# A decoder layer on one core: units laid out by a table, and VectorE asks for three kinds of results one or two search rounds later

## The chip, the cores and the metric

The kernel runs on one core of a Trainium2 chip. The time is the device time of one execution in microseconds (us); shown are the median of three runs, and one execution recorded by the hardware profiler. The engines are TensorE (PE in the rows; PEld are its weight loads), VectorE (DVE), ScalarE (ACT), GpSimd (POOL) and SyncE (SP), which here only starts transfers. Each works through its own list of instructions in order and waits on semaphores for the others.

## What is computed

A decoder layer over 8 sequences of 512 rows of 512 numbers, in fp32: causal self attention with a normalization of each query and key head, cross attention of 16 heads in which each query row keeps only its 32 largest scores, and a gated MLP with quantized activations and ternary weights. Cut to what matters:

```python
x = x + attn(layernorm(x))            # 16 heads of 32, q and k normalized per head, causal softmax
x = x + xattn(layernorm(x), ctx)      # scores; top_k(scores, 32); softmax over them; times V; @ Wo.T
x = x + ffn(layernorm(x))             # 512 -> 2048 -> 512
def ffn(x):
    gate, up = silu(bitlinear(x, w_gate)), bitlinear(x, w_up)
    return bitlinear(gate * up, w_down)
def bitlinear(x, w):                  # rows scaled by max|x|, rounded to 127 steps; w to -1, 0, 1
    return act_quant(x) @ weight_quant(w).T
```

## The kernel before

After a setup of the weights (to about 140 us) the kernel is one long software pipeline written by hand. Its step is the **slot**, numbered `s` from -7 to 161. In a slot the self attention works on one query tile of 128 rows for a group of 4 heads, and the cross attention on another: self attention of item `s`, cross attention of item `c = s - LAG`, 20 slots later. A batch (sequence) is 16 slots, 4 head groups of 4 query tiles; `s % 4` is the query tile, and with the causal mask its scores grow from 128 to 512 columns.

**TensorE.** A slot has 8 cells (0 to 7), even ones for a self head, odd ones for a cross head. In each cell TensorE transposes the probabilities of the item before (`probs`, L593), makes the scores of a new one (`scores`, L625 to L630) and multiplies the last turned probabilities with V (`values`, L607). `cells(s)` (L120) then appends **units** to a cell: `self_qkv` (L682, four per group), `cross_v` (L694), `cross_kT` and `cross_qT` (L701), `self_kT` and `self_qT` (transposes), the output projections `self_oT`, `self_out`, `cross_oT`, `cross_out` (L654), the turned rows `feed` and `x2T`, and of the MLP `gate` and `up` (L662, four chunks of 512 per row tile, chunk 0 to 3), `hT` (L635) and `down` (L670). Units share two PSUM banks in turn; a unit waits until the unit two before it has been read.

**VectorE.** It finds the 32 largest scores of each row by search rounds: MAX8 gives the eight largest (L876), MATCH_REPLACE8 takes them out (L881). Each slot is two halves of two heads; a half is FIRST_MAX, ROUND_1, ROUND_2 (a replacement and a maximum for each of its heads) and ROUND_3 (with one more replacement). Between the rounds stand its other duties, in a written order: `self_maxima` (L1013), `sum_squares` (L1005), `norms` (the weighted sums of both attentions, divided by their weights, L898 and L907; it waits for TensorE's last sum of the slot before), `mlp` (maximum of a chunk of gate times up, L965; a chunk is **early** if its gate and up stand in cell 2, **late** if in cell 6, and a late one's maximum is taken in the next slot), `down` (L983), `row_scale`, `cross_rows` (adds `cross_out` to the rows, L924) and `self_rows` (adds `self_out`, L937).

**ScalarE** copies each result out of PSUM and takes the exponentials, `rest_exp` (L825) after the last replacement of a half. **GpSimd** makes the negative maxima as biases (`cross_bias` L1175, `self_bias` L1182), gate times up (`silu`, L1109 to L1115), the differences of exponentials (L1168), the quantization of the chunks (`inner_quant`, L1127), and in slots with `s % 4 == 2` the head norm (a power, L1147).

**SyncE** goes through the slots too: feeds of rows, `x1`, `x2` and residual rows, weights of a group (one buffer for both attentions), then 32 copies of the turned keys and queries into their stacks (L513), which the first scores of a group need.

The MLP of a batch follows its cross attention. **Table numbers** below count slots from the batch's first cross slot: slot number 26 is `s = LAG + 16*b + 26`, in which the next batch's cross attention is at 10. Before, `cross_tile` (projection of tile t) is at 15 + t, chunks 0, 1 of tile t at 17 + 3t, chunks 2, 3 at 18 + 3t, and `hT` with `down` at 19 + 3t. `self_tile` is the self attention's projection, for a batch two ahead at numbers 26 to 29.

## Time and profile before

| | |
|---|---|
| median of 3 runs | 3904.87 us (3895.12 to 3911.36) |
| profiled execution | 3917.24 us, its span 3915.5 us |
| mean granted TensorE clock | 0.867 of full speed |
| busy: PE, PEld | 3310.2 us (85%), 2433.7 us (62%) |
| busy: DVE, ACT, POOL | 3220.0 us (82%), 2451.7 us (63%), 1917.9 us (49%) |

The span has four parts: setup to about 140 us; self attention alone until VectorE's first search at 490.7 us; the searches of 128 items until 3771 us; and the last projections and MLP tiles. Busy time says how much an engine works, not what holds it up; for that one reads what ended each idle time. The granted clock is 1 at 2.4 GHz and 0.5 at 1.2 GHz, so a mean of 0.92 is 16% of the time at the lower level.

### The profile page before, as it was taken

To read this page: it belongs to the slowest core of one execution; us is meant where nothing else is said; L and a number is where in the kernel's file an instruction comes from. 1 tells how busy PE (TensorE), PEld (TensorE's weight loads), DVE (VectorE), ACT (ScalarE), POOL (GpSimd) and SP (SyncE) were. 2 spreads that over 40 slices of the span, in tenths; PEclk is the share of its full clock that TensorE was granted. 3 is DMA by queue.
4 is the path that set the end of the run, shared out by engine and by line. 5 is a ranking of instruction groups with operands and counts; after the bars stand their busy time and mean duration, and the time that the engine had idled before them with its cause. 6 is when DMAs were issued, how large, how long until landed. Compare 5 with 4: busy or idle time off the path is not lost.

```text
span 3915.5 us, 61337 instructions
## 1 busy us (share of the span) xinstructions
PE 3310.2 (85%) x18502; PEld 2433.7 (62%) x18502; DVE 3220.0 (82%) x7571; ACT 2451.7 (63%) x4921; POOL 1917.9 (49%) x2444
## 2 busy tenths in 40 slices
PE   1577888999989998999999989999899988877765
PEld 1355567766666676667667667667666766554542
DVE  4311189999989999899989998999989998999961
ACT  2344466676777677667766677767666776555533
POOL 0122334446555466546654655546554654355445
PEclk7677878898999989988989999988998898887768
DMA  8112232232223222322223222322233221211100
GB/s 279 46 49 65 80 84 73 74 82 75 51 76 88 75 69 79 84 79 74 76 72 84 75 52 74 87 76 67 79 88 83 65 71 41 62 46 36 33 22 19
DMA packets 167443, 283.04 MB, mean 72 GB/s; under 512 B 40639, under 2 KB 52939, under 8 KB 166606
## 3 DMA queue, kind: packets, MB, share of 16 engines
q1 hardware_dynamic: 160782, 275.98, 25.9%
q10 hardware_dynamic: 6336, 3.15, 0.3%
q8 instruction: 153, 2.51, 0.3%
q14 instruction: 172, 1.41, 0.1%
HBM read 113.27 MB, written 31.46 MB: 37 GB/s over the span
## 4 chain that ended last, share of the span: by engine, by line
DVE 33%; PE 32%; POOL 11%; issue 8%; ACT 6%; SPq 4%; DMA 1%; DVEq 0%; POOLq 0%; ACTq 0%
DVE cW L881 15%; DVE top L876 12%; PE bank L682 6%; PE bank L607 6%; PE bank L654 5%; SPq L513 4%; PE bank L593 3%; PE bank L670 2%; PE bank L701 2%; PE bank L635 2%; POOL hh L1111 2%; POOL srs L1147 2%; POOL hh L1115 2%; PE bank L694 2%; DVE smx L1013 2%
## 5 line engine op out<-in xcount | busy, mean ns | idle before, releaser
L881 DVE MATCH_REPLACE8 cW<-top,cW 128x512 f32<-128x512 f32 x1536 | 1026.3, 676 | 0.0
L876 DVE MAX8 top<-cW 128x8 f32<-128x512 f32 x1536 | 980.7, 680 | 0.0
L1168 POOL TENSOR_TENSOR cS<-cS,cW 128x512 f32<-128x512 f32 x512 | 642.2, 1276 | 233.2 <-ACT cW L825 232.7
L797 ACT ACTIVATE PT<-bank 128x512 f32<-128x512 f32 (+3 forms) x1024 | 538.0, 525 | 314.4 <-PE bank L593 310.6
L607 PE MATMUL bank<-cv,PT 128*128 128x33 f32 x4096 | 586.0, 290 | 121.8 <-ACT PT L797 120.6
L607 PEld LDWEIGHTS bank<-cv,PT 128*128 128x128 f32 x4096 | 555.0, 210 | 157.0 <-ACT PT L797 151.0
L1175 POOL TENSOR_SCALAR cnb<-top 128x2 f32<-128x2 f32 x256 | 49.3, 193 | 871.6 <-DVE top L876 857.9
L607 PEld LDWEIGHTS bank<-sv,PT 128*128 128x128 f32 x2560 | 398.7, 211 | 77.7 <-ACT PT L797 55.4
L825 ACT ACTIVATE cW<-cW,cnb 128x512 f32<-128x512 f32 x512 | 347.8, 734 | 127.6 <-DVE cW L881 127.2
L819 ACT ACTIVATE cS<-cS,cnb 128x512 f32<-128x512 f32 x512 | 380.1, 742 | 46.9 <-POOL cnb L1175 24.0
L682 PE MATMUL bank<-w_group,xT 128*128 128x384 f32 x1024 | 403.3, 541 | 0.0
L607 PE MATMUL bank<-sv,PT 128*128 128x33 f32 x2560 | 374.5, 281 | 32.4 <-ACT PT L797 31.5
L1013 DVE TENSOR_REDUCE smx<-sP 128x2 f32<-128x256 f32 (+3 forms) x256 | 205.7, 804 | 225.9 <-ACT sP L806 225.9
L593 PE MATMUL bank<-ident,cS 128*128 128x128 f32 x2048 | 346.2, 296 | 0.0
L881 DVE MATCH_REPLACE8 cW<-top,cS 128x512 f32<-128x512 f32 x512 | 342.1, 676 | 0.3 <-issue 0.3
L876 DVE MAX8 top<-cS 128x8 f32<-128x512 f32 x512 | 327.0, 680 | 7.6 <-ACT cS L806 7.6
L806 ACT ACTIVATE cS<-bank 128x512 f32<-128x512 f32 x512 | 312.7, 611 | 1.8 <-PE bank L630 1.8
L812 ACT ACTIVATE sP<-sP,snb 128x384 f32<-128x384 f32 (+3 forms) x512 | 294.1, 577 | 28.3 <-POOL snb L1182 27.3
L593 PEld LDWEIGHTS bank<-ident,cS 128*128 128x128 f32 x2048 | 279.5, 162 | 46.0 <-issue 23.5
L682 PEld LDWEIGHTS bank<-w_group,xT 128*128 128x128 f32 x1024 | 201.7, 207 | 133.9 <-issue 34.2
L593 PE MATMUL bank<-ident,sP 128*128 128x128 f32 x1280 | 254.6, 301 | 35.8 <-ACT sP L812 34.8
L1161 POOL TENSOR_TENSOR part<-part 128x512 fp32r<-128x512 f32 x128 | 163.1, 1274 | 243.1 <-ACT part L740 242.8
(151 smaller groups left out, 6131.8 us busy)
## 6 DMA issues: line engine op xcount, KB each, us to landing
sk_stack<-part SPq DMA_DIRECT2D x512, 64.0 KB, 2.0
sq_stack<-part SPq DMA_DIRECT2D x512, 64.0 KB, 2.0
ck_stack<-part SPq DMA_DIRECT2D x512, 64.0 KB, 2.0
cq_stack<-part SPq DMA_DIRECT2D x512, 64.0 KB, 2.0
w_group<-wa_by_group SPq DMA_DIRECT2D x32, 768.0 KB, 4.8
w_group<-wc_by_group SPq DMA_DIRECT2D x32, 768.0 KB, 4.3
feed<-in_x SPq DMA_DIRECT2D x32, 256.0 KB, 3.0
feed<-in_ctx SPq DMA_DIRECT2D x32, 256.0 KB, 3.0
```

Source lines behind the costliest of these rows:

```text
L593: mm = pe.transpose(turned_ps[C.parity("turned_full", label)][:, k * P:(k + 1) * P], p[:, k * P:(k + 1) * P], ident[:])
L607: mm = pe.matmul(o[:, j * (HD + 1):(j + 1) * (HD + 1)], pt[:, k * P:(k + 1) * P], v[m // NT % len(v)][:, k, j, :], start=k == 0, stop=k == ...
L682: mm = pe.matmul(ps[:, 0:3 * P], xT[:, c, t * P:(t + 1) * P], w_group[:, c, :], start=False, stop=c == NC - 1, skip_group_check=True)
L797: act.activation(PT[k][:, 0:n], turned_ps[k][:, 0:n], ACT.Copy).then_inc(turned_read, step("turned_read", label))
L806: act.activation(dst, score_ps[k][:, 0:n], ACT.Copy).then_inc(score_read, step("score_read", label))
L812: act.activation(p, p, ACT.Exp, bias=snb[:, j:j + 1], scale=SCALE).then_inc(sexp, step("sexp", (m, j)))
L819: act.activation(cS[c % 2][j][:], cS[c % 2][j][:], ACT.Exp, bias=cnb[c % 2][:, j:j + 1], scale=SCALE).then_inc(cexp, step("cexp", (c, j)))
L825: act.activation(cW[j][:], cW[j][:], ACT.Exp, bias=cnb[c % 2][:, j:j + 1], scale=SCALE).then_inc(crest, step("crest", (c, j)))
L876: dve.max(top8[:, j, r, :], src[:]).then_inc(topk, step("topk", (c, r, "max", j)))
L881: dve.match_replace(cW[j][:], top8[:, j, r, :], src[:], REPLACED).then_inc(topk, step("topk", (c, r, "replace", j)))
L1013: dve.reduce_max(smx[:, 2 * half:2 * half + 2], sP[half][:, :, 0:n], AXX).then_inc(smax, step("smax", (s, half)))
L1168: pool.tensor_tensor(cS[m % 2][j][:], cS[m % 2][j][:], cW[j][:], ALU.subtract).then_inc(cprob, step("cprob", (m, j)))
```

## The change

The places of the units come from a function `schedule(b)` with lists of table numbers, and so do `hT` (now `mlp_inner`) and `down`, which may be in different slots. For most batches `cross_tile` is at 15, 17, 18, 19, the 16 chunks are spread over 20 to 33 (one or two a slot, some slots with none), `hT` is at 22, 25, 30, 35 and `down` at 23, 25, 30, 37. The last two batches keep groups of three slots a tile. The first `self_qkv` of a group moves from cell 0 to cell 5 of the slot before; others move by a cell. On VectorE the second self maximum moves behind ROUND_1, `norms` behind ROUND_2, `cross_rows` behind ROUND_3, the first self maximum behind ROUND_1 and `self_rows` behind ROUND_2 of the second half. GpSimd's late `silu` goes ahead of the self bias, ScalarE's first two cross exponentials one cell earlier. SyncE's row transfers move behind the stack copies, their loads a slot ahead. The amount of work is the same: VectorE has 3961 merged rows in either kernel.

```diff
+def schedule(b):
+
+    def dense(first):
+        chunks = [(first + 3 * t + r, early) for t in range(NT) for r in range(2) for early in (True, False)]
+        ends = tuple(first + 3 * t + 2 for t in range(NT))
+        return chunks, ends, ends
+    if b == NB - 1:
+        return ((15, 16, 17, 18), *dense(17))
+    if b == NB - 2:
+        return ((15, 17, 18, 19), *dense(20))
+    chunks = [(20, True), (20, False), (21, True), (21, False), (22, False), (23, True), (24, True), (24, False),
+              (26, True), (27, True), (29, True), (29, False), (31, True), (32, True), (32, False), (33, True)]
+    return (15, 17, 18, 19), chunks, (22, 25, 30, 35), (23, 25, 30, 36 if b == NB - 3 else 37)
...
+def planned(s, part, entry, tiles=NT):
+
+    out = []
+    for b in range(NB):
+        for i, at in enumerate(schedule(b)[part]):
+            if at == entry(s - LAG - SLOTS * b):
+                out.append(tiles * b + i)
+    return out
...
 def cells(s):
 
     u = [[] for _ in range(CELLS)]
-    g, q = self_group(s), s % NT
+    q = s % NT
+    g = s // NT + 2
+    if q == 3 and 0 <= g < NGROUPS:
+        u[5].append(("self_qkv", g, 0))
+    g = self_group(s)
     if g is not None:
-        for at, cell, unit in ((0, 0, ("self_qkv", g, 0)), (0, 3, ("self_qkv", g, 1)), (0, 6, ("self_qkv", g, 2)),
-                               (1, 1, ("self_qkv", g, 3)), (3, 2, ("self_kT", g)), (3, 3, ("self_qT", g))):
+        for at, cell, unit in ((0, 2, ("self_qkv", g, 1)), (0, 5, ("self_qkv", g, 2)),
+                               (1, 0, ("self_qkv", g, 3)), (3, 2, ("self_kT", g)), (3, 3, ("self_qT", g))):
             if at == q:
                 u[cell].append(unit)
     g = cross_group(s)
     if g is not None:
-        for at, cell, unit in ((1, 5, ("cross_v", g)), (2, 0, ("cross_kT", g)), (2, 3, ("cross_qT", g))):
+        for at, cell, unit in ((1, 5, ("cross_v", g)), (2, 0, ("cross_kT", g)), (2, 4, ("cross_qT", g))):
             if at == q:
                 u[cell].append(unit)
     if cross_tile(s) is not None:
         u[0].append(("cross_oT", cross_tile(s)))
         u[1].append(("cross_out", cross_tile(s)))
     if x1_tile(s) is not None:
-        u[1].append(("feed", "x1", x1_tile(s)))
+        u[2].append(("feed", "x1", x1_tile(s)))
     if self_tile(s) is not None:
-        u[2].append(("self_oT", self_tile(s)))
-        u[3].append(("self_out", self_tile(s)))
+        u[4].append(("self_oT", self_tile(s)))
+        u[5].append(("self_out", self_tile(s)))
     if x2_tile(s) is not None:
         u[4].append(("x2T", x2_tile(s)))
+    for t in mlp_inner(s):
+        for n in range(NF):
+            u[3 + n].append(("hT", t, n))
...
                     for s in slots:
                         c = s - LAG
                         top(c, 0, FIRST_MAX)
+                        top(c, 0, ROUND_1)
                         self_maxima(s - 1, 1)
-                        top(c, 0, ROUND_1)
                         sum_squares(s)
-                        norms(s)
                         mlp(s - 1, False)
                         down(s - 1)
                         top(c, 0, ROUND_2)
+                        norms(s)
                         row_scale(s)
+                        top(c, 0, ROUND_3)
                         cross_rows(s)
-                        top(c, 0, ROUND_3)
                         top(c, 1, FIRST_MAX)
+                        top(c, 1, ROUND_1)
                         self_maxima(s, 0)
-                        self_rows(s)
-                        top(c, 1, ROUND_1)
                         feed_stats_of(s + 1)
                         top(c, 1, ROUND_2)
+                        self_rows(s)
                         mlp(s, True)
                         top(c, 1, ROUND_3)
...
                         cross_bias(c, 0)
+                        silu(s - 1, False)
                         self_bias(s - 1, 1)
-                        silu(s - 1, False)
                         for j in (2, 3):
                             probability(c - 1, j)
                         low_parts(now[0] + now[1] + now[2])
                         rows_quant(s)
                         inner_quant(s - 1)
                         head_norm(s)
-                        low_parts(now[3])
+                        low_parts(now[3] + now[4])
...
                         elif k == 1:
+                            cross_exp(c, 0)
+                        elif k == 2:
+                            cross_exp(c, 1)
                             self_exp(s - 1, 2)
-                        elif k == 2:
+                        elif k == 3:
                             self_exp(s - 1, 3)
-                            cross_exp(c, 0)
-                        elif k == 3:
-                            cross_exp(c, 1)
```

VectorE in the slot of table number 29, from the second half's first maxima (cS_2 and cS_3 are the scores of its two heads, cW what is left of them); before:

```order
L876 MAX top<-cS_2 128x8
L876 MAX top<-cS_3 128x8
L1013 TENSOR_REDUCE smx<-sP 128x2
L937 TENSOR_TENSOR xres<-bank,xres 128x512
L940 BN_STATS x1stat<-xres 128x6
L944 BN_AGGR x1mv<-x1stat 128x2
L881 MATCH_REPLACE cW<-top,cS_2 128x512
L881 MATCH_REPLACE cW<-top,cS_3 128x512
L876 MAX top<-cW 128x8 x2
```

and now:

```order
L901 MAX top<-cS_2 128x8
L901 MAX top<-cS_3 128x8
L906 MATCH_REPLACE cW<-top,cS_2 128x512
L906 MATCH_REPLACE cW<-top,cS_3 128x512
L901 MAX top<-cW 128x8 x2
L1038 TENSOR_REDUCE smx<-sP 128x2
L906 MATCH_REPLACE cW<-top,cW 128x512 x2
L901 MAX top<-cW 128x8 x2
L962 TENSOR_TENSOR xres<-bank,xres 128x512
L965 BN_STATS x1stat<-xres 128x6
L969 BN_AGGR x1mv<-x1stat 128x2
L990 TENSOR_REDUCE hmx<-hh 128x1
```

The self maximum moved behind one round and the addition of `self_out` (xres) behind two; an early chunk's maximum (hmx) follows it.

TensorE in the same slot, around `self_out` (wproj, oT); before, from its bias on:

```order
L651 MATMUL bank<-bias,ones 128x512
L654 MATMUL bank<-wproj,oT 128x512 x4
L593 MATMUL bank<-ident,sP 128x128
L625 MATMUL bank<-sk_stack,sq_stack 128x256
L627 MATMUL bank<-mask,ident 128x128
L607 MATMUL bank<-cv,PT 128x33 x4
L593 MATMUL bank<-ident,cS_2 128x128 x4
L630 MATMUL bank<-ck_stack,cq_stack 128x512
L607 MATMUL bank<-sv,PT 128x33
L692 MATMUL bank<-bias,ones 128x128
L694 MATMUL bank<-w_group,ctxT 128x128 x4
```

and now, up to it (three more pairs of L717 and L719 are left out):

```order
L655 MATMUL bank<-ck_stack,cq_stack 128x512
L632 MATMUL bank<-sv,PT 128x33
L717 MATMUL bank<-bias,ones 128x128
L719 MATMUL bank<-w_group,ctxT 128x128 x4
...
L676 MATMUL bank<-bias,ones 128x512
L679 MATMUL bank<-wproj,oT 128x512 x4
```

`cross_v` (w_group, ctxT) stood behind `self_out` and stands ahead of it now, as do the transposes, scores and sums of cells 4 and 5.

GpSimd at the start of the slot of table number 25, where a late chunk is due (th and hh are the gated product, cnb and snb the biases of the cross and the self exponentials); before:

```order
L1175 TENSOR_SCALAR cnb<-top 128x2
L1182 TENSOR_SCALAR snb<-smx 128x2
L1109 TENSOR_SCALAR th<-th 128x512
L1111 TENSOR_TENSOR hh<-th,hh 128x512
L1115 TENSOR_TENSOR hh<-hh,uc 128x512
L1168 TENSOR_TENSOR cS_2<-cS_2,cW 128x512
```

and now:

```order
L1200 TENSOR_SCALAR cnb<-top 128x2
L1134 TENSOR_SCALAR th<-th 128x512
L1136 TENSOR_TENSOR hh<-th,hh 128x512
L1140 TENSOR_TENSOR hh<-hh,uc 128x512
L1207 TENSOR_SCALAR snb<-smx 128x2
L1193 TENSOR_TENSOR cS_2<-cS_2,cW 128x512
```

The self bias moved behind the product.

## Rows read from the trace of the kernel before

**Rows 1.** The page: span, busy time, clock by slice, ScalarE's last exponentials (mean ns).

```profile
span 3915.5 us, 61337 instructions
...
PE 3310.2 (85%) x18502; PEld 2433.7 (62%) x18502; DVE 3220.0 (82%) x7571; ACT 2451.7 (63%) x4921; POOL 1917.9 (49%) x2444
...
PEclk7677878898999989988989999988998898887768
...
L825 ACT ACTIVATE cW<-cW,cnb 128x512 f32<-128x512 f32 x512 | 347.8, 734 | 127.6 <-DVE cW L881 127.2
```

**Rows 2.** Windows, one batch: length, busy PE, PEld, DVE, ACT, POOL; clock, DMA, GB/s.

```profile
2155.00:2578.00 423.00, 387.20 (x2282) 287.26 (x2281) 393.70 (x930) 296.56 (x606) 239.60 (x304) 0.92 0.28 75
```

**Rows 3.** Waits of VectorE, 2155.4 to 2577.7: us in total, times, longest.

```profile
DVE xres L937 <- PE bank L654: 11.5, 4, 8.1
DVE hmx L965 <- POOL hh L1115: 7.0, 9, 1.8
DVE rr L898 <- issue: 6.0, 4, 2.2
DVE x2t L924 <- issue: 2.6, 1, 2.6
```

**Rows 4.** Timeline of VectorE, number 26: start, us, instruction, [idle before it].

```profile
2411.36 1.28 DVE L876 MAX8 top<-cS 128x8 f32<-128x512 f32 x2
...
2420.03 1.28 DVE L876 MAX8 top<-cW 128x8 f32<-128x512 f32 x2
...
2422.54 1.28 DVE L876 MAX8 top<-cW 128x8 f32<-128x512 f32 x2
...
2435.28 0.69 DVE L937 TENSOR_TENSOR xres<-bank,xres 128x512 f32<-128x512 f32 x1 [8.11 <-PE bank L654]
```

**Rows 5.** Timeline of TensorE, numbers 25 and 26.

```profile
2396.62 1.09 PE L635 MATMUL bank<-ident,hh 128*128 128x128 f32 x4 [2.85 <-POOL hh L1127]
...
2402.52 2.08 PE L694 MATMUL bank<-w_group,ctxT 128*128 128x128 f32 x8
...
2408.01 1.16 PE L694 MATMUL bank<-w_group,ctxT 128*128 128x128 f32 x8
...
2415.82 0.38 PE L593 MATMUL bank<-ident,sP 128*128 128x128 f32 x2
...
2427.62 3.68 PE L701 MATMUL bank<-x1T,w_group 128*128 128x512 f32 x8
...
2431.55 3.70 PE L654 MATMUL bank<-wproj,oT 128*128 128x512 f32 x8
```

**Rows 6.** Timeline of GpSimd and VectorE, a late chunk in number 27.

```profile
2448.75 0.62 POOL L1109 TENSOR_SCALAR th<-th 128x512 f32<-128x512 f32 x1
...
2450.80 1.28 POOL L1115 TENSOR_TENSOR hh<-hh,uc 128x512 f32<-128x512 f32 x1
...
2452.11 0.69 DVE L965 TENSOR_REDUCE hmx<-hh 128x1 f32<-128x512 f32 x1 [0.57 <-POOL hh L1115]
```

**Rows 7.** Timelines of GpSimd, TensorE and VectorE, numbers 22 and 23.

```profile
2324.25 5.43 POOL L1147 TENSOR_TENSOR srs<-srs,minus_half 128x32 f32<-128x32 f32 x1
...
2335.06 5.11 PE L670 MATMUL bank<-wdT,hT 128*128 128x512 fp8e4 x16 [5.08 <-ACT hT L740]
...
2342.20 0.21 DVE L898 RECIPROCAL rr<-bank 128x8 f32<-128x8 f32 x1 [1.78 <-issue]
```

**Rows 8.** TensorE before the first search: its waits, 230 to 490; timeline near 300.

```profile
PE bank L625 <- DMA sq_stack<-part: 12.1, 4, 4.2
...
302.91 0.44 PE L625 MATMUL bank<-sk_stack,sq_stack 128*128 128x128 f32 x1 [4.14 <-DMA sq_stack<-part]
...
303.85 4.50 PE L682 MATMUL bank<-w_group,xT 128*128 128x384 f32 x8
```

**Rows 9.** Waits of VectorE, 526 to 920, and 3325 to 3770.

```profile
DVE xres L937 <- PE bank L654: 8.2, 3, 4.0
...
DVE hmx L965 <- POOL hh L1115: 11.5, 10, 4.5
```

More of the change, by code:

```diff
@@ L147, in cells @@
     for t in mlp_down(s):
-        for n in range(NF):
-            u[3 + n].append(("hT", t, n))
         u[7].append(("down", t))
@@ L437, in pipeline @@
                         C.plan("pool_rows", ("ln", t, k))
-                for t in mlp_down(s - 1):
-                    C.plan("h_dve", ("out", t))
                 for early, at in ((False, s - 1), (True, s)):
+                    for t in mlp_down(s - 1) if early else ():
+                        C.plan("h_dve", ("out", t))
                     for t, n in mlp_chunk(at, early):
@@ L556, in _ @@
                                 copy_part(unit, j)
+                        t = cross_tile(s)
+                        if t is not None:
+                            sp.wait_ge(dve_rows, upto("dve_rows", ("x2", t)))
+                            sp.dma_start(rows(x2_rows, t), x2t[:]).then_inc(x2_out, step("x2_out", t, 16))
+                        t = cross_tile(s + 1)
+                        if t is not None:
+                            if t:
+                                sp.wait_ge(dve_rows, upto("dve_rows", ("x2", t - 1)))
+                            sp.wait_ge(x1_out, upto("x1_out", t, 16))
+                            sp.dma_start(x1res[:], rows(x1_rows, t)).then_inc(x1res_in, step("x1res_in", t, 16))
+                        t = self_tile(s)
+                        if t is not None:
+                            sp.wait_ge(x1_stats, upto("x1_stats", ("x1", t)))
+                            sp.dma_start(rows(x1_rows, t), xres[:]).then_inc(x1_out, step("x1_out", t, 16))
                         for t in mlp_down(s - 1):
                             store_y(t)
+                        for t in mlp_down(s + 1):
+                            sp.wait_ge(x2_out, upto("x2_out", t, 16))
+                            if t:
+                                sp.wait_ge(y_out, upto("y_out", t - 1, 16))
+                            sp.dma_start(x2res[:], rows(x2_rows, t)).then_inc(x2res_in, step("x2res_in", t, 16))
+                        t = self_tile(s + 1)
+                        if t is not None:
+                            if t:
+                                sp.wait_ge(x1_out, upto("x1_out", t - 1, 16))
+                                sp.wait_ge(x1_norm, upto("x1_norm", (t - 1, 4)))
+                            sp.dma_start(xres[:], rows(x_rows, t)).then_inc(xres_in, step("xres_in", t, 16))
                     sp.wait_ge(x1_out, 16 * NTILES)
```

43 lines of the change are left out of this document (7 added, 36 removed).

## The prediction

> **What bounds the kernel now.** The page comes first: TensorE is busy for 85% of the span and VectorE for 82%, and the granted clock, in tenths by slice, is well below full in the first and the last stretch and near it between [rows 1]. The windows say it by stage. In one batch of the middle (422.3 us, 16 slots from the search of table number 20 on) VectorE is busy 393.7 us, TensorE 387.2 at a mean clock of 0.92, ScalarE 297 and GpSimd 240 [rows 2]. Neither of the first two is full, and their loads are almost equal, but TensorE's units are spread unevenly over the slots, so in some of them one waits for the other. The table of waits of that batch shows what VectorE waits for: 11.5 us for `self_out` (L937, 8.1 of it in one slot), 7.0 for the gated product (L965), 6.0 for the weighted sums (L898), 2.6 for `cross_out` (L924): 27.1 us, 6.4% of the batch [rows 3]. A VectorE without waits would need 395 us a batch; that is the most the change can reach, about 28 x 5.7 = 155 us over the middle.
>
> The timelines say why `self_out` is late. At table number 26 VectorE starts the slot at 2411.36, asks 15.8 us later (2435.28 less 8.11) and gets it at 23.9 [rows 4]. One slot earlier TensorE waited 2.85 us for the quantized rows of the MLP (hT, which needs the last chunk's maximum and then GpSimd), fell to the lower clock, ran part of `cross_v` at 2.08 us instead of 1.16 a block, and so began slot 26 at 2415.8, 4.5 us behind VectorE; there `cross_qT` (3.68) and `self_out` (3.70 plus its bias) end at 2435.25 [rows 5].
>
> **The change, part by part.** No instruction is added or removed; I cost places. Slots are called by their number in the table (26 is ten slots after 16).
>
> *VectorE's questions.* A search round on two heads takes 2.51 us (2420.03 to 2422.54) [rows 4]. Weighted sums (`norms`) are asked one round later, `cross_rows` one longer round (3.8 us) later, `self_rows` two rounds (5.0 us) later.
> - `norms`: its waits were 6.0 us in 4 places, none over 2.2 [rows 3]. A round covers 2.51. Gone: -6.0.
> - `cross_rows`: 2.6, covered by 3.8. But its slot 31 now follows a slot with MLP tail work (below), and TensorE comes some 4 us late; I leave 1.3. -1.3.
> - `self_rows`: asked 5.0 us later, but on TensorE `self_out` moves from cell 3 to cell 5, and `cross_qT` and `self_oT` to cell 4. In between lie the transposes, scores and sums of cells 4 and 5, 2.6 us by their places in the PE timeline. Slot 25 on TensorE holds the same units as before, hT and `down` included, so I expect the 2.85 us wait and the late start of 4.5 us again: end at 23.9 + 2.6 = 26.5, less 0.1, against a question at 15.8 - 0.5 (the wait for the sums) + 5.0 = 20.3. Wait 6.1 instead of 8.1. Slots 27 and 28: `self_qkv` (4.5 us at the lower clock [rows 8], some 3 at the higher) now stands ahead of `self_out` in cell 5. ScalarE copies for the first cross sum only after two exponentials of 0.73 us that end VectorE's last slot [rows 1], so TensorE is there no earlier than 2.1 us into the slot; adding the units up from there gives 19.5 to 20 against questions at 18.4 to 19: 1.1 and 1.4. Slot 29: `cross_v` (4 x 1.16 and biases, 5.05) stands ahead of `self_out` where before it stood behind it, and a gate and up chunk (2.1) is there too; TensorE ends at 22.5 against a question at 17.9: 4.7. Sum 13.3 instead of 11.5: +1.8. Bounds: 2.8 if TensorE starts each of these slots at its earliest, 20 if slot 27 is held up as well.
>
> *The gated product.* GpSimd makes it in 3.3 us from th (2448.75) to the end of the last product (2452.08), VectorE gets it at 2452.11 after 0.57 us of waiting [rows 6].
> - Late chunks: GpSimd now starts them right behind cnb, before the self bias, so they are ready 5.0 us into the slot. VectorE asks after max, round and self maximum, at 4.0 to 4.6; `norms` (0.7) no longer stands ahead. Waits of 0.9 three times and 0.4 once where no sum of squares (1.2) covers it: 3.1.
> - Early chunks: GpSimd starts them behind the self bias, which needs the self maximum; that is now one round later, and only one round (2.51) lies between it and the question. 3.75 - 2.51 = 1.24 us of waiting in slots 20, 24, 31, 32, 33, 0.4 in 23, nothing where `self_rows` or the feed statistics lie between (21, 26, 27, 29). 6.6. Before, self rows or two rounds (5.0) covered it.
> - Together 9.7 instead of 7.0: +2.7. With VectorE late for other reasons it could be 5, with TensorE late 13.
>
> *The table.* Adding the mean durations of its lines, a slot's units now take TensorE 23 to 26 us; before it was 18 to 34. `down` of tile 0 moves a slot behind hT; before, hT and `down` in slot 22 met GpSimd's 5.43 us power, the bias that ScalarE needed came late, and TensorE stood 5.08 us before `down`, then VectorE 1.78 [rows 7]. That knot leaves 22, but 30, also a slot with the power, now has hT and `down` of tile 2. This is in the numbers for `norms` and `cross_rows` above.
>
> A batch: -6.0 - 1.3 + 1.8 + 2.7 = -2.8 us. The middle from 900 to 3300 us has 5.7 batches: -16.
>
> *The beginning.* Until 490 us TensorE has only self attention. It waits 12.1 us in four slots for the stack's transfers; one is 4.14 us at 302.91, and a `self_qkv` of 4.9 us follows [rows 8]. That unit moves ahead of the wait, into cell 5 of the slot before, and fills it. `cross_qT` one cell later delays the first search by 2. -12 + 2 = -10. If the transfers start later too, 0; if latencies behind it shorten as well, -20. The first batch of searches has no MLP yet, its 8.2 us for `self_out` [rows 9] fall to about 3, and some 2 of `cross_rows` go: -7.
>
> *The end of the searches.* From 3325 to 3770 us VectorE waits 11.5 us in ten places for the product [rows 9]. With no self attention early chunks cost nothing, but each of ten late ones loses the 0.7 us cover of `norms`: +7, less 2 to 3 for `cross_rows`: +4. The last 145 us keep their order: 0.
>
> *SyncE.* The row transfers now stand behind the stack copies and a slot ahead of their use. The copies can only start sooner, and a row is asked for some 15 us after its transfer may start: 0. Uncovered it would show as a DMA wait, at most 2 us as now.
>
> *Sum.* -16 - 10 - 7 + 4 = -29. The profiled execution took 3917.2 us (span 3915.5 [rows 1]), 12 above the median of 3904.9: 3888 for it, 3876 as a median.
>
> **A rule weighed.** The granted clock is 0.92 in the middle, and the blocks of `cross_v` took 2.08 us at the lower and 1.16 at the higher level, after 2.85 us of idleness [rows 2, 5]. The Trainium skill, "TensorE: Matmul & The Clock Gate", Part 1, says that the throttled clock is the default and that activity lifts it. By that rule a levelled table would buy clock, and with it time in just the slots where TensorE is late. The trace agrees on the direction; the sum above goes by the rows, which keep the wait in slot 25.
>
> **The rivals.**
> - *TensorE is on time* (0.22). Levelled slots and a higher clock let it start slots 26 to 29 with VectorE: `self_out` waits fall from 13.3 to the lower bound of 2.8. For: questions 5 us later, and no ScalarE exponential is held up behind a waiting VectorE, since the first replacement now precedes `self_rows`. Against: slot 25 unchanged. 10.5 x 5.7 = 60 more: 3815.
> - *The cover moves and nothing is won* (0.25). The beginning's transfers come later or `self_out` in slots 27 and 29 costs 2 us more than I say; then the middle gains nothing: 3890 to 3915, within half a percent.
> - *Slower* (0.15). The knot at slot 30: hT, quantization and the 5.43 us power in one GpSimd slot, then low parts and stack copies late, so ScalarE holds TensorE in 31, and `cross_out` of 31 and hT follow late. In the trace such a slot cost VectorE 0.5 + 1.8 + 1.4; if it also costs `cross_out` 3 us in each of 31 and 33, a batch pays 9.7, 55 in all: 3930. It decides once TensorE starts 31 more than 7 us late.
>
> **How the numbers follow.** My forecast is a small gain, 0.3 to 2%: chance 0.38 for it. Half a percent, 19.5 us, is what a measurement of this kernel can tell. Faster: 0.38 less a little for its near edge, plus 0.22: 0.59. Same: 0.26. Slower: 0.15. The range goes from below the on-time case, 3795, to the slower case, 3930; about 0.08 lies below and 0.1 above. The likeliest case by itself: 3840 to 3893.
>
> **What would show it.** In a middle batch: no wait at the reciprocal; `self_out` still waited for, some 6 us at 26 and 4 to 5 at 29, with `cross_v` ahead; the gated product waited for about ten times, 1.2 us each in early chunks outside 26 to 29; length 419 to 421 us against 423. VectorE's first search near 480 us instead of 490.7. A `down` wait of 5 us in slot 30, none in 22. I am wrong if `self_out` waits vanish (table better than I think), or if the first search doesn't come sooner, or if TensorE's waits at 31 grow past 7 us.

## The result, and the profile after

The changed kernel took 3981.99 us (median of 4 runs, 3972.75 to 3988.54) against 3905.38: a ratio of 1.0197, 95% interval 1.0166 to 1.0228. It is about 2% slower, clear of noise, where a median of 3876 us was forecast, and it lies above the range of 3795 to 3930.

The page of the changed kernel (to be read against [rows 1]) shows the same busy times in a longer span: VectorE 3220.5 us as against 3220.0, so on VectorE all that was lost is waiting.

```profile
span 3983.8 us, 61337 instructions
...
PE 3340.1 (84%) x18502; PEld 2427.1 (61%) x18502; DVE 3220.5 (81%) x7571; ACT 2447.8 (61%) x4921; POOL 1918.9 (48%) x2444
...
PEclk7777788898899999998899889998999988887778
```

VectorE's first maxima of an item mark its way. First search: 490.7 us before, 480.7 after. From item 0 to 16: 394.7 us, now 399.2. Items 16 to 96: 2115.6, now 2164.7. Items 96 to the end: 768.8, now 793.4. So -10.0, +4.5, +49.1, +24.6; behind the searches nothing changes. The five batches from item 16 to 96 are not alike: they lose 0.0, 10.0, 16.4, 14.6 and 8.1 us. The one looked at below (items 64 to 80) is the fourth.

One batch of the middle (windows; to [rows 2], length 423) and VectorE's waits in it (us in total, times, longest; to [rows 3]):

```profile
2176.30:2613.20 436.90, 394.47 (x2280) 288.56 (x2280) 393.20 (x930) 295.41 (x606) 239.72 (x305) 0.91 0.27 73
```

```profile
DVE hmx L990 <- POOL hh L1140: 23.1, 11, 3.6
DVE xres L962 <- PE bank L679: 8.3, 4, 3.4
DVE x2res L1008 <- PE bank L695: 5.3, 2, 3.6
DVE x2t L949 <- DMA x1res<-x_rows: 3.4, 1, 3.4
DVE x2t L949 <- issue: 0.8, 1, 0.8
DVE smx L1038 <- ACT sP L831: 0.5, 1, 0.5
```

The sums (rr) are gone from the list, `self_out` has fallen from 11.5 to 8.3, and the gated product has risen from 7.0 to 23.1. The count, 11 waits, is about the ten forecast; the sizes are not: five are of the sizes forecast (0.90 to 1.22) and six are of 2.45 to 3.59. Some of them in VectorE's timeline (start, us, instruction, idle before it):

```profile
2306.10 0.69 DVE L990 TENSOR_REDUCE hmx<-hh 128x1 f32<-128x512 f32 x1 [3.59 <-POOL hh L1140]
...
2347.89 0.69 DVE L990 TENSOR_REDUCE hmx<-hh 128x1 f32<-128x512 f32 x1 [3.55 <-POOL hh L1140]
...
2422.13 0.69 DVE L990 TENSOR_REDUCE hmx<-hh 128x1 f32<-128x512 f32 x1 [1.20 <-POOL hh L1140]
2431.56 0.69 DVE L990 TENSOR_REDUCE hmx<-hh 128x1 f32<-128x512 f32 x1 [0.90 <-POOL hh L1140]
```

The 1.20 and 0.90 (numbers 24 and 25) are the terms of the prediction to a few hundredths. The 3.59 (number 20) is TensorE's: a slot with `s % 4 == 0` now has a `self_qkv` in cell 2, ahead of the early gate. It took 5.49 us there, the lower clock level by its length; the next one (2307.32) took 2.85:

```profile
2294.70 5.49 PE L707 MATMUL bank<-w_group,xT 128*128 128x384 f32 x8
2299.98 1.38 PE L687 MATMUL bank<-wgT,x2T 128*128 128x512 fp8e4 x4
```

The 3.55 (number 22) is GpSimd's. VectorE began that slot at 2338.84; GpSimd's timeline has three normalizations of fed rows behind one another, and only then the bias and the late product, which starts 5.7 us into the slot (the last of the three, and what follows):

```profile
2343.40 0.77 POOL L1076 TENSOR_SCALAR feed<-feed,fcol 128x512 f32<-128x512 f32 x1
2344.26 0.19 POOL L1200 TENSOR_SCALAR cnb<-top 128x2 f32<-128x2 f32 x1
2344.53 0.62 POOL L1134 TENSOR_SCALAR th<-th 128x512 f32<-128x512 f32 x1
2345.23 1.27 POOL L1136 TENSOR_TENSOR hh<-th,hh 128x512 f32<-128x512 f32 x1
2346.58 1.28 POOL L1140 TENSOR_TENSOR hh<-hh,uc 128x512 f32<-128x512 f32 x1
```

The other four long waits have two causes. In numbers 21 (2.59) and 23 (2.45, a late chunk) GpSimd is free and waits for ScalarE's copy of gate and up, since TensorE is late. In 23 (2.49, an early chunk) and 31 (3.03), both with `s % 4 == 3`, GpSimd's low parts of the turned self keys and queries stand ahead of the bias and the product, and wait for ScalarE. GpSimd's timeline, number 23:

```profile
2371.33 0.62 POOL L1134 TENSOR_SCALAR th<-th 128x512 f32<-128x512 f32 x1 [2.15 <-ACT hh L765]
...
2388.18 1.28 POOL L1186 TENSOR_TENSOR part<-part 128x512 fp32r<-128x512 f32 x1 [4.68 <-ACT part L765]
```

`hT` of number 22 waits for its late product in TensorE, 5.22 us; before, it waited 1.82 there and `down` behind it the 5.08 of [rows 7]. Another wait in TensorE is new, and no term had it. The first `self_qkv` of a group stands in the very slot in which its weights are asked for; TensorE's timeline at number 23, and SyncE's:

```profile
2352.90 1.09 PE L660 MATMUL bank<-ident,hh 128*128 128x128 f32 x4 [5.22 <-POOL hh L1152]
...
2395.07 0.47 PE L704 MATMUL bank<-bias,ones 3*128 3x128 bf16 x3 [5.65 <-issue]
```

```profile
2385.73 0.43 SPq L513 DMA_DIRECT2D w_group<-wa_by_group  x1
```

```profile
w_group<-wa_by_group SPq DMA_DIRECT2D x1, 768.0 KB, 9.3
```

This load took 9.3 us from issue to landing (the self attention's loads 5.0 in the median), so it landed at 2395.0, just ahead of the unit; the wait is called "issue" there, but it ends with the load. There are five such waits from 900 to 3300 us, one a batch and 25.4 us in all, each behind a load that took 7.6 to 9.3 us.

### The profile page after: what moved, and what is told of

It is laid out like the page before. It is cut to its first block, busy times and chain, and to the rows that moved or that the text cites. A ratio compares the mean times of both kernels' runs of the same rounds, so it can differ in the third digit from the quotient of the medians.

```text
span 3983.8 us, 61337 instructions
## 1 busy us (share of the span) xinstructions
PE 3340.1 (84%) x18502; PEld 2427.1 (61%) x18502; DVE 3220.5 (81%) x7571; ACT 2447.8 (61%) x4921; POOL 1918.9 (48%) x2444
## 3 DMA queue, kind: packets, MB, share of 16 engines
q1 hardware_dynamic: 160782, 275.98, 25.4%
## 4 chain that ended last, share of the span: by engine, by line
PE 28%; DVE 26%; POOL 16%; issue 11%; ACT 9%; SPq 5%; DMA 2%; DVEq 0%; POOLq 0%; ACTq 0%
DVE cW L906 12%; DVE top L901 9%; PE bank L707 6%; SPq L538 5%; PE bank L632 5%; PE bank L679 3%; POOL hh L1136 3%; PE bank L618 2%; PE bank L726 2%; POOL srs L1172 2%; POOL hh L1140 2%; PE bank L695 2%; PE bank L660 2%; POOL cS L1193 2%; PE bank L719 2%
## 5 line engine op out<-in xcount | busy, mean ns | idle before, releaser
L632 PEld LDWEIGHTS bank<-sv,PT 128*128 128x128 f32 x2560 | 388.5, 207 | 82.2 <-ACT PT L822 60.8
L707 PE MATMUL bank<-w_group,xT 128*128 128x384 f32 x1024 | 424.5, 564 | 0.0
L1207 POOL TENSOR_SCALAR snb<-smx 128x2 f32<-128x2 f32 x256 | 49.3, 193 | 525.5 <-DVE smx L1038 521.7
L707 PEld LDWEIGHTS bank<-w_group,xT 128*128 128x128 f32 x1024 | 211.7, 218 | 145.1 <-issue 54.6
```

Source lines behind the costliest of these rows:

```text
L632: mm = pe.matmul(o[:, j * (HD + 1):(j + 1) * (HD + 1)], pt[:, k * P:(k + 1) * P], v[m // NT % len(v)][:, k, j, :], start=k == 0, stop=k == ...
L707: mm = pe.matmul(ps[:, 0:3 * P], xT[:, c, t * P:(t + 1) * P], w_group[:, c, :], start=False, stop=c == NC - 1, skip_group_check=True)
```

## The experiments

Each ran beside the kernel before, and the ratio is to that. Waits are those of 900 to 3300 us. Eleven of the eighteen times fell outside every range that was set for them beforehand, four of these by less than 5 us: the parts do not add up simply.

**The orders without the table.**

```diff
 def schedule(b):
-    if b == NB - 1:
-        return ((15, 16, 17, 18), *dense(17))
+    return ((15, 16, 17, 18), *dense(17))
```

> The changed kernel with the old places of the MLP's chunks, hT, down and cross_tile (three slots a tile from number 17, cross_tile at 15 to 18) for every batch; all orders on VectorE, GpSimd, ScalarE and SyncE and the other units' cells as changed. Theory A, the orders cost (the questions for the gated product are badly covered, and rows asked for later hold PSUM banks): stays slow, 3950 to 3990 us. Theory B, the table costs (it puts late chunks behind the feed rows' norms on GpSimd and down where VectorE waits): back to 3880 to 3910 us, with the 10 us of the earlier first search kept.

3994.1 us, 1.0214 (1.0188 to 1.0239), with 133.8 us of waits for the product (105.1 in the changed kernel): the loss is there without the table. It is that of the orders and the new cells together; no run has the new cells alone.

**The table without the orders.** Cells and the orders of VectorE, ScalarE and GpSimd as before; of the change only `schedule(b)` with what reads it, and SyncE's order.

```diff
 def cross_tile(s):
-    return tile_at(s, LAG + 15)
+    return next(iter(planned(s, 0, lambda at: at)), None)
...
+def mlp_inner(s):
+    return planned(s, 2, lambda at: at)
```

> The kernel before with only the new table (chunks, hT, down, cross_tile) and the changed order of SyncE; cells of the other units and the orders of VectorE, GpSimd and ScalarE as before. Theory A, the orders cost: 3890 to 3910 us or less. Theory B, the table costs: 3950 to 3990 us.

3926.2 us, 1.0047 (1.0030 to 1.0064). A small loss of its own, with a wait that the kernel before hardly had:

```profile
DVE x2t L945 <- DMA x1res<-x_rows: 41.8, 6, 8.8
```

**The same with SyncE's order as before.** From this order in the kernel above

```diff
-                        for at, which, g, before in loads:
...
-                        t = cross_tile(s + 1)
+                        t = x1_tile(s)
...
+                        t = cross_tile(s)
...
+                        for at, which, g, before in loads:
```

to row transfers ahead of weights and stack copies, and in the slot of their use.

> The kernel before with the new table of the MLP and the cross tiles alone, SyncE's order as before. With the table and SyncE's new order it took 3926 us and waited 41.8 us for the residual rows x1res. If those waits are SyncE's order: they vanish, and the time is 3880 to 3895 us, faster than before. If they are only the last of several things that come late together: 3920 to 3930 us.

3932.4 us, 1.0058 (1.0041 to 1.0075), and the wait for x1res is still 40.6 us. SyncE's order is not its cause. The load of tile t's row waits until `cross_out` of t - 1 is added, and the table has tiles 1 to 3 in slots 17, 18, 19, each shortly behind the last; that this is the cause was argued and not tried.

**SyncE's order as before in the changed kernel, alone and with the early maximum later.**

> The changed kernel with SyncE's row transfers at their old places, ahead of the stack copies; all else as changed. Theory S (the residual rows stand behind 32 copies and come late): VectorE's 15 us of waiting for x1res between 900 and 3300 us vanish, and the time falls by 10 to 30 us, to 3950 to 3970 us. Theory N (SyncE's order costs nothing by itself, since VectorE would wait a moment later for TensorE anyway): within 10 us of the changed kernel's 3982.

> The changed kernel with the early chunk's maximum asked behind ROUND_3 of the second half and SyncE's row transfers at their old places. If the two costs add (52 us for the product, 10 to 30 for the rows): 3900 to 3920 us. If SyncE's order costs nothing: 3930 us, as with the maximum's place alone.

3975.9 us, 1.0174 (1.0157 to 1.0190), and 3926.7 us, 1.0037 (1.0016 to 1.0058). Both intervals overlap those of the kernels with the new order. No cost of SyncE's order shows; nothing was forecast for it.

**The early chunk's maximum asked behind the last round.**

```diff
-                        mlp(s, True)
                         top(c, 1, ROUND_3)
+                        mlp(s, True)
```

> The changed kernel with VectorE's maximum of an early chunk asked one round later, behind ROUND_3 of the second half. Theory A: the 1.2 us waits of the early chunks (five a batch) and most of those of 2.5 to 3 us go, 35 to 60 us faster than the changed kernel (3925 to 3945). If these waits only show that TensorE is late, they return elsewhere: under 15 us faster.

3929.7 us, 1.0058 (1.0039 to 1.0077): one moved line gives back 52 of the 77 us. VectorE's product waits (after, then this kernel):

```profile
DVE hmx L990 <- POOL hh L1140: 105.1, 62, 3.6
```

```profile
DVE hmx L990 <- POOL hh L1140: 47.7, 29, 4.4
```

**The late one and `down` behind ROUND_2 as well.**

```diff
-                        mlp(s - 1, False)
-                        down(s - 1)
                         top(c, 0, ROUND_2)
+                        mlp(s - 1, False)
+                        down(s - 1)
```

> The changed kernel with the early maximum behind ROUND_3 of the second half, and the late maximum and down's addition behind ROUND_2 of the first half. With the early one alone it took 3930 us and still waited 48 us for the product and 18 for down between 900 and 3300 us. If cover is what is missing: most of these 66 us go, 3870 to 3890 us. If what is behind (the inverse scale and with it the quantized rows, hT and down) then comes late in TensorE: 3920 to 3960 us.

3914.1 us, 1.0008 (0.9995 to 1.0021). The product's waits are 13.6 us, but `self_out` has 75.3 (53.2 in the changed kernel) and `cross_out` 20.5 (6.4), so some of what was freed is spent on TensorE's rows. The changed kernel, mended so, is as good as the one before and no better.

**GpSimd's feed norms behind the late product.**

```diff
-                        feed_ln(s + 1)
...
                         silu(s - 1, False)
                         self_bias(s - 1, 1)
+                        feed_ln(s)
```

> The changed kernel with GpSimd's norms of the feed rows moved from the end of a slot to behind the late product and the self bias of the next. Theory of the feed norms (three of them, 6.9 us, stand ahead of the late product of number 22, where VectorE waits 3.6 us, and delay head norm, hT and down behind it): the 3.6 us go and with them most of the waits in 23 and 24 (3.6 for down), 30 to 50 us faster than the changed kernel. If the lateness is TensorE's own: under 15 us.

4009.2 us, 1.0257 (1.0232 to 1.0282): the theory fell. The product's waits fell only from 105.1 to 93.7 us. The three norms then hold the difference of exponentials instead, and with it the next replacement and the transposes. VectorE has a new wait for that, and TensorE's longest for the quantized rows goes from 6.7 to 12.2 us:

```profile
DVE cW L906 <- POOL cS L1193: 23.9, 10, 5.2
```

```profile
PE bank L660 <- POOL hh L1152: 61.2, 11, 12.2
```

**The self maxima at their old place in the changed kernel.**

```diff
-                        top(c, 0, ROUND_1)
                         self_maxima(s - 1, 1)
+                        top(c, 0, ROUND_1)
...
-                        top(c, 1, ROUND_1)
                         self_maxima(s, 0)
+                        top(c, 1, ROUND_1)
...
-                        silu(s - 1, False)
                         self_bias(s - 1, 1)
+                        silu(s - 1, False)
```

> The changed kernel with both self maxima asked before ROUND_1 again, and GpSimd's self bias ahead of the late product again; all else as changed. Theory P (the product is late because the self bias ahead of it waits for a later question): the early products get their 2.5 us back, VectorE's waits for the gated product between 900 and 3300 us fall from 105 to 50 to 65 us, and the time to 3925 to 3945 us. Theory T (the product is late because TensorE and ScalarE deliver the chunk late by the table): little changes, 3970 to 3990 us.

3964.6 us, 1.0133 (1.0106 to 1.0160), product waits 67.4 us. It gives back 17 us where theory P had 37 or more: `self_out` (64.6) and the self maxima themselves (22.3, from 1.3) take a part.

**Self maxima as before and both product questions later.** The edits of self_first and both_behind together.

> The changed kernel with both self maxima and the self bias at their old places, and both product questions late (early behind ROUND_3, late and down behind ROUND_2). The product's lateness as in both_behind (3914 us), and self exponentials 2.5 us sooner for TensorE. If the parts add, 17 us less than both_behind: 3890 to 3900 us. If TensorE and its rows bound, as in both_behind: 3905 to 3920 us.

3902.5 us, 0.9976 (0.9960 to 0.9992): product waits 2.0 us, `self_out` 78.8. That is 12 us less than both_behind, where self_first had given 17.

**The row questions at their old places in the changed kernel.**

```diff
+                        norms(s)
                         mlp(s - 1, False)
                         down(s - 1)
                         top(c, 0, ROUND_2)
-                        norms(s)
                         row_scale(s)
-                        top(c, 0, ROUND_3)
                         cross_rows(s)
+                        top(c, 0, ROUND_3)
                         top(c, 1, FIRST_MAX)
+                        self_rows(s)
```

(and `self_rows` no longer behind ROUND_2).

> The changed kernel with norms, cross_rows and self_rows asked at their old places (self maxima still late); all else as changed. Theory B (a later question holds one of TensorE's two PSUM banks, since a projection's bank is free only when VectorE has added it; in the changed kernel TensorE waits 29.8 and 14.7 us for the bank behind cross_out and 25.4 us behind self_out): those waits vanish, and VectorE's waits for norms, cross_out and self_out come back; the two about cancel, 3970 to 4000 us. Theory C (the later questions are a pure gain of cover): VectorE loses the 34 us of norms and some 60 us of self_out cover again, 4030 us or more.

4208.3 us, 1.076 (1.0734 to 1.0785); its profiled execution was far from the timed ones, so no row of it is shown. With the new cells, in which `self_out` stands two cells later, the later questions save 226 us. The expectation was wrong in one thing: the 25.4 us before the `self_qkv` bias are the weights' load (above), not a held bank.

**One part of the change at a time in the kernel before: the row questions.**

```diff
-                        norms(s)
                         mlp(s - 1, False)
                         down(s - 1)
                         top(c, 0, ROUND_2)
+                        norms(s)
                         row_scale(s)
-                        cross_rows(s)
                         top(c, 0, ROUND_3)
+                        cross_rows(s)
                         top(c, 1, FIRST_MAX)
                         self_maxima(s, 0)
-                        self_rows(s)
                         top(c, 1, ROUND_1)
                         feed_stats_of(s + 1)
                         top(c, 1, ROUND_2)
+                        self_rows(s)
                         mlp(s, True)
```

> The kernel before with one part of the change alone: norms asked behind ROUND_2, cross_rows behind ROUND_3 and self_rows behind ROUND_2 of the second half. With the cells as they were, theory C (later questions are cover) says that VectorE's waits for the weighted sums (34 us between 900 and 3300 us), for cross_out (18) and most of those for self_out (64) go: 3820 to 3860 us. Theory B (an unread projection holds a PSUM bank, and TensorE waits in VectorE's place) says that TensorE pays most of it back: 3880 to 3910 us.

3937.9 us, 1.0068 (1.0053 to 1.0083): slower, not faster. VectorE's waits, before and then with this part:

```profile
DVE xres L937 <- PE bank L654: 63.6, 21, 8.1
DVE hmx L965 <- POOL hh L1115: 41.9, 51, 2.9
DVE rr L898 <- issue: 34.2, 22, 3.1
DVE x2t L924 <- issue: 13.2, 5, 2.8
```

```profile
DVE hmx L965 <- POOL hh L1115: 111.2, 69, 4.6
DVE x2res L983 <- PE bank L670: 26.5, 7, 5.1
DVE xres L937 <- PE bank L654: 17.3, 6, 4.2
DVE x2t L924 <- PE bank L654: 11.3, 11, 1.6
DVE x2t L924 <- issue: 7.1, 5, 1.9
```

The rows' waits fall by 80 us (5.0 for x1res, not shown above, included), and product and `down` gain 96. The waits for rows had been the product's cover.

**The self maxima alone.** 

```diff
-                        self_maxima(s - 1, 1)
                         top(c, 0, ROUND_1)
+                        self_maxima(s - 1, 1)
...
-                        self_maxima(s, 0)
                         top(c, 1, ROUND_1)
+                        self_maxima(s, 0)
...
+                        silu(s - 1, False)
                         self_bias(s - 1, 1)
-                        silu(s - 1, False)
```

> The kernel before with one other part alone: both self maxima asked behind ROUND_1, GpSimd's late product ahead of the self bias. If the later self bias alone uncovers the early products: about 1.2 us in nine early chunks of a batch that self_rows does not cover, 60 us in all, 3950 to 3970 us. If the old cells deliver the chunks early enough: within 10 us of 3905.

4006.8 us, 1.0237 (1.0217 to 1.0256): the dearest single part, 97 us. ScalarE's waits for the self bias, before and then here, show a price that the prediction had not seen at all:

```profile
ACT sP L812 <- POOL snb L1182: 7.9, 13, 0.6
```

```profile
ACT sP L812 <- POOL snb L1182: 115.0, 48, 5.0
```

**The same with ScalarE's self exponentials a cell later, as in the change.**

```diff
                         elif k == 1:
+                            cross_exp(c, 0)
+                        elif k == 2:
+                            cross_exp(c, 1)
                             self_exp(s - 1, 2)
-                        elif k == 2:
+                        elif k == 3:
                             self_exp(s - 1, 3)
-                            cross_exp(c, 0)
-                        elif k == 3:
-                            cross_exp(c, 1)
```

> The self maxima moved as in maxima_late (4007 us), and ScalarE's self exponentials one cell later, behind the cross exponentials, as in the changed kernel. In maxima_late ScalarE waited 115 us for the self bias between 900 and 3300 us, 8 us before. If that wait, with the cross work queued behind it, is the price: it falls to about 20 us and the time to 3920 to 3950 us. If the price is the product behind the bias on GpSimd: 3990 to 4010 us.

3982.9 us, 1.0186 (1.0167 to 1.0206). ScalarE's wait falls to 37.7 us and 24 us come back. So at least a quarter of the 97 us is ScalarE held at the head of its queue; the product (68.9, 41.9 before) and `self_out` (80.2, 63.6 before) still wait longer. The Trainium skill, "PSUM — Partial Sum Buffer", Engine vs sequencer instructions, says that ScalarE's queue is a strict FIFO. The trace agrees: the same exponentials, put one cell later in that queue, took 77 us from its waits.

**The product questions alone, in the kernel before.**

```diff
-                        mlp(s - 1, False)
-                        down(s - 1)
                         top(c, 0, ROUND_2)
+                        mlp(s - 1, False)
+                        down(s - 1)
...
-                        mlp(s, True)
                         top(c, 1, ROUND_3)
+                        mlp(s, True)
```

> The kernel before with the product's questions alone moved: the late chunk's maximum and down's addition behind ROUND_2 of the first half, the early chunk's behind ROUND_3 of the second. If VectorE's 42 us of waiting for the product between 900 and 3300 us are simply lost time: 3860 to 3875 us. If they are passed on to the rows of TensorE (self_out, cross_out, sums), which come no sooner: 3890 to 3915 us.

3879.7 us, 0.9925 (0.9903 to 0.9946): 30 us faster. The product's 41.9 us of waits are gone from the list, the sums' are up from 34.2 to 47.9.

**Rows and product together.** As rows_late, and `mlp(s - 1, False)` with `down` behind ROUND_2, `mlp(s, True)` behind ROUND_3.

> The kernel before with the questions for rows (norms, cross_rows, self_rows) and for the product both moved later, self maxima and cells as before. Rows alone took 3938 us: waits for rows fell from 116 to 36 us between 900 and 3300 us, and those for the product rose from 42 to 111 and for down from 0 to 27. Theory U (the row waits had covered the product, and a later question for it makes the gain real): some 120 us of the 138 of product and down go, 3820 to 3850 us. Theory V (TensorE, at 91% of this stretch, is what bounds; a wait moves from one place to the next): 3890 to 3920 us.

3839.0 us, 0.9816 (0.9796 to 0.9836): 71 us faster. The part that cost 28 us alone is worth 41 once the product is covered. VectorE's waits:

```profile
DVE hmx L965 <- POOL hh L1115: 27.8, 24, 2.0
DVE xres L937 <- PE bank L654: 25.0, 16, 4.4
DVE x2res L983 <- PE bank L670: 16.1, 5, 3.2
DVE x2t L924 <- issue: 12.3, 5, 2.9
```

**And the first `self_qkv` ahead, or the table, on top of that.** The first has this edit, the second VectorE's order of rows_prod in table_sp.

```diff
+    q = s % NT
+    g = s // NT + 2
+    if q == 3 and 0 <= g < NGROUPS:
+        u[5].append(("self_qkv", g, 0))
+    g = self_group(s)
...
-        for at, cell, unit in ((0, 0, ("self_qkv", g, 0)), (0, 3, ("self_qkv", g, 1)), (0, 6, ("self_qkv", g, 2)),
+        for at, cell, unit in ((0, 3, ("self_qkv", g, 1)), (0, 6, ("self_qkv", g, 2)),
```

> As rows_prod (3839 us, the best so far), and the first self_qkv of a group in cell 5 of the slot before, as in the changed kernel, where the first search came 10 us sooner (480.7 instead of 490.7 us). If that start is a gain of its own: about 3829 us with the first search near 480 us. If a batch pays for the unit in a fuller cell (it stands ahead of work that VectorE waits for): 3840 us or more.

> As rows_prod, with the new table of the MLP and the cross tiles in place of the old one, SyncE's order as before. The table alone cost 22 us (3932 instead of 3910), with 41 us of waiting for x1res and 33 for the product. If the later questions cover its waits too, a levelled table is worth something: below 3835 us. If its own waits (x1res behind the stored x2 rows, tiles 1 to 3 close together at 17, 18, 19) can't be covered by a round: 3850 to 3870 us.

The unit ahead: 3845.8 us, 0.9848 (0.9828 to 0.9868), no gain; VectorE's waits for the self scores go from 5.1 to 27.4 us. The table: 3825.9 us, 0.9797 (0.9778 to 0.9815), the fastest kernel here, 80 us less than before and 156 less than the changed one. The table alone had cost 22 us. Its interval touches that of rows_prod, so a gain of the table over it is likely and not shown.

Set beside self_both (3902.5 us), this kernel shows a cost that no single experiment isolated. Both have the same table, the same order on VectorE to the last line, and the self bias ahead of the product. They differ in the new cells, ScalarE's order of the exponentials, SyncE's order, and which low parts GpSimd makes in the middle of the slot. The one with these parts as changed takes 77 us more (70 by the ratios), and the intervals (0.9960 to 0.9992, 0.9778 to 0.9815) are far apart. Taking SyncE's order back moved the medians by 6 us, once up and once down, and the first `self_qkv` ahead by 7; which of the others makes the rest is not shown. VectorE's waits for `self_out` and for the self scores, in self_both and in rp_table (all its waits are 151 and 84 us):

```profile
DVE xres L962 <- PE bank L679: 78.8, 21, 6.8
DVE smx L1038 <- ACT sP L831: 27.7, 10, 5.0
```

```profile
DVE xres L958 <- PE bank L675: 19.8, 18, 5.1
DVE smx L1034 <- ACT sP L827: 5.2, 6, 1.0
```

TensorE's waits at the beginning, 230 to 490 us, in the changed kernel and in rp_qkv (to [rows 8]):

```profile
PE bank L632 <- ACT PT L822: 14.7, 33, 1.0
...
PE bank L650 <- DMA sq_stack<-part: 3.0, 2, 1.5
```

```profile
PE bank L611 <- ACT PT L801: 25.3, 43, 6.7
...
PE bank L629 <- DMA sq_stack<-part: 1.3, 1, 1.3
```

## Why the prediction was wrong

The sum was -2.8 us for a middle batch; its length went from 422.3 to 436.9, +14.6, and VectorE's waits in it from 27.1 to 41.4. (That stretch starts at number 16 of its batch, not at 20 as the prediction has it, and 28 x 5.7 is 160; the 155 is 27.1 x 5.7. Neither enters the sum.)

- **The step that failed** is "Together 9.7 instead of 7.0: +2.7" for the gated product: 23.1, so +16.1. The shortfall of a question that finds its producers on time was right (1.20, 0.90). Wrong was that producers are on time: the sum added the new places on VectorE to a GpSimd and a TensorE that start with VectorE. It left out that a `self_qkv` stands ahead of the gate in cell 2 (3.59), the feed norms ahead of the late product (3.55), the low parts ahead of the early one (2.49, 3.03), and that TensorE comes late with the late ones (2.59, 2.45). Late chunks waited 10.4 us where the sum had 3.1, early ones 12.7 where it had 6.6. early_behind shows what the wait is worth: 57 us less of it, 52 us less time. With the late question and `down`'s moved too (both_behind) the loss is gone. self_first shows that the trade is not one for one: 38 us less of it, 17 us less time.
- **"Gone: -6.0"** for the sums was right at its place (no such wait in the batch) and wrong as a gain. rows_late shows why: the wait stood ahead of the product's question and covered it. The prediction took 0.7 us, the work of `norms`, as the cover lost, where it was the work and the wait. rows_prod shows that the gain is real once the product has another cover.
- **`self_out`**: 8.3 instead of the 13.3 forecast. The 2.85 us wait in slot 25 did not come back: TensorE began slot 26 at 2450.74, 0.4 us behind VectorE instead of 4.5, and the wait there is 2.14 instead of 6.1. The term was too dear by 5 us. But that is beside the kernel before; rp_table against self_both suggests that the new cells, counted here as 2.6 us of delay, cost more than any term had, and which part of them is open.
- **`down`** "5 us in slot 30, none in 22": on TensorE 1.44 us ahead of `down` of slot 30, and 2.66 for its `hT`; VectorE waits 3.6 in 24 and 1.8 in 31. The slot-30 rival, with 9.7 us of waiting a batch there, named the wrong place. The knot did not leave 22: `hT` waits 5.22 us there.
- **ScalarE's wait for the self bias** was no term. The change as a whole avoids most of it (21.6 us), since it moved the exponentials too; alone the move costs 97 us.
- **TensorE's banks.** Later questions leave a result in its bank, and nothing was costed for it. TensorE waited 4.5 us for `cross_out`'s addition ahead of the turned self keys and queries before, 14.7 now, and 29.8 more ahead of gate and up, where before had no such row. rp_table, the fastest, has 14.7 and 16.7 of the two, so it is no main cause.
- **Beginning**: -10.0, as forecast, by the wrong step. In rp_qkv the moved unit removed the transfers' waits (10.9 to 1.3 us), and the first search came only 1.7 us sooner than in rows_prod (488.0 and 489.7), for the waits for turned probabilities grew in their place (20.9 to 25.3). The changed kernel has 14.7 of these, 22.4 before, and so has maxima_exp, which came only 2.6 us sooner (488.1). In the nine traces with all the new cells (that of rows_old left out) the first search is at 473.3 to 484.4 us, in the ten without them at 483.8 to 491.5, so it most likely comes from the new cells together; which of them is open.
- **First batch** forecast -7, measured +4.5: `self_out` waits were 11.1 us, not 3. **End of the searches**: the +4 was for 3325 us on. From item 109 on (3339.3 before, 3385.8 now) it is +22, nearly all of the +24.6. Without self attention early chunks were free as forecast, and late ones waited 1.21 us instead of 0.8. The +7 for the product was right (11.5 to 18.9 us); wrong was "less 2 to 3 for `cross_rows`": VectorE's waits at the addition of `cross_out` went from 2.2 to 10.1 us, 5.7 of it for x1res. The rest of the 22 is open.
- **The rule weighed.** The clock of the batch went from 0.92 to 0.91, though by the rule that the prediction took from the Trainium skill, "TensorE: Matmul & The Clock Gate", Part 1, that activity lifts the clock, a levelled table was to buy some. That doesn't speak against the rule, since TensorE had more waits (245 us from 900 to 3300, 202 before). Between 900 and 3300 us it was 0.92 before, 0.91 after, 0.89 in maxima_late and 0.93 in rp_table.
- **The rivals.** "Slower" had 0.15 and a place that was not the one. Two rivals were missing: that of a question whose cover is the wait being removed, and that of new cells that cost more than their place in the list says.

## What to carry to other kernels

A wait in an in-order queue hides the lateness of everything asked behind it. Before counting a wait as a gain, ask of the next two questions when their producers start, and whether these start with the waiting engine: here 80 us of removed waits came back as 96. Move the questions behind a removed wait along with it (28 us of loss alone, 71 of gain together), and place a result that another engine's queue needs first (a bias at the head of ScalarE's work) as early as it can be. And once one part of a change has been mended, compare two mended kernels that differ in the rest alone: only self_both beside rp_table shows some 70 us that belong to the new cells and what was moved with them.

## What the runs showed of the hardware

In the changed kernel a 768 KB weights load (`w_group`) took from 4.1 to 9.3 us to land. The longest is the one at 2385.73, ahead of which SyncE had issued a residual row and three feeds, 256 KB each, within 1.8 us. The trace's row, min, median and max of 64 such loads (32 for each attention):

```profile
DMA to landing us min/median/max: 4.1/4.4/9.3
```

The reader of the longest waited 5.65 us.
